# In the drain of a routed MoE pipeline, the down products of the last unit but one are put in front of the gate/up products of the last unit

## What is computed

```
xn = layernorm(x)
s  = RWKV attention(xn): three time-mixed projections, a scan over time, output product with Wo
# MoE with 16 experts, top 4, hidden size 256:
probs = softmax(xn @ w_router.T); top_w, top_e = top_k(probs, 4); top_w /= sum|top_w|
for e in range(16):
    h = silu(xn @ w_gate[e]) * (xn @ w_up[e])
    ffn += coeff_e * (h @ w_down[e])          # coeff_e = 0 where e isn't chosen
out = x + s * silu(ffn)
```

## Time and profile before

| | value |
|---|---|
| median of 3 runs | 324.53 us |
| the profiled execution | 324.29 us, span 322.5 us |
| PE busy | 287.6 us (89%) |
| DVE busy | 251.2 us (78%) |
| ACT busy | 146.0 us (45%) |
| POOL busy | 203.7 us (63%) |
| chain that ended last | PE 60%, DVE 16%, DMA 12% |

### The profile page before, as it was taken

How to read it: one execution, slowest core, us unless ns; L and a number is a source line. 1 busy time by engine, 2 the same in 40 slices (tenths; PEclk the granted TensorE clock), 3 DMA queues, 4 the chain that set the end, 5 groups by cost and what they waited for, 6 DMA issues and landing times.

```text
span 322.5 us, 4601 instructions
## 1 busy us (share of the span) xinstructions
PE 287.6 (89%) x1298; PEld 212.3 (66%) x1299; DVE 251.2 (78%) x523; ACT 146.0 (45%) x219; POOL 203.7 (63%) x201
## 2 busy tenths in 40 slices
PE   0698969979889999999999999999999999969960
PEld 0443424434335665888888888888888888848850
DVE  2889799986986888689299896898869961439993
ACT  1791726423267752841935536465273232312140
POOL 3600089993773767778778787787777776242281
PEclk9999979999999999999999999999999999988995
DMA  7896000016377676459655454655556578899798
GB/s 230 285 374 287 0 1 1 0 34 244 99 236 273 226 272 218 146 212 291 217 199 170 149 213 148 227 160 192 171 168 207 155 221 301 265 337 303 223 230 163
DMA packets 30379, 63.28 MB, mean 196 GB/s; under 512 B 4332, under 2 KB 20205, under 8 KB 30192
## 3 DMA queue, kind: packets, MB, share of 16 engines
q10 hardware_dynamic: 7568, 23.88, 21.2%
q0 software_dynamic: 8544, 19.41, 21.2%
q1 hardware_dynamic: 14240, 19.66, 18.1%
HBM read 50.35 MB, written 15.20 MB: 203 GB/s over the span
## 4 chain that ended last, share of the span: by engine, by line
PE 60%; DVE 16%; DMA 12%; issue 4%; ACT 3%; POOL 3%; ACTq 1%; SPq 0%; DVEq 0%; POOLq 0%
PE ps L589 52%; DMA rows<-wgu_in 5%; PE ps L696 4%; DVE arena L848 3%; DVE ohB L1007 2%; DMA y_rows<-arena,dst_idx 2%; PE ps L599 2%; DVE ohA L1002 2%; DMA wrou<-wrouT_in 1%; DMA rows<-y_rows 1%; DVE arena L1136 1%; DMA y_rows<-arena,late 1%; POOL arena L393 1%; POOL y_rows L400 1%; DVE arena L1103 1%
## 5 line engine op out<-in xcount | busy, mean ns | idle before, releaser
L589 PE MATMUL ps<-arena,rows 128*128 128x256 f32 x448 | 102.8, 384 | 3.1 <-DMA rows<-wgu_in 3.1
L393 POOL DMA_INDIRECT arena<-xn_rows,tok_idx x72 | 79.6, 1106 | 26.2 <-issue 21.6
L589 PEld LDWEIGHTS ps<-arena,rows 128*128 128x128 f32 x448 | 84.1, 193 | 13.9 <-issue 3.5
L400 POOL DMA_INDIRECT y_rows<-arena,dst_idx x60 | 65.2, 1086 | 26.2 <-issue 16.5
L589 PE MATMUL ps<-wdn,arena 128*128 x288 | 67.8, 380 | 0.4 <-DVE arena L1036 0.4
L589 PEld LDWEIGHTS ps<-wdn,arena 128*128 128x128 f32 x288 | 54.2, 191 | 7.7 <-issue 0.8
L589 PE MATMUL ps<-arena 128*128 128x512 f32 x96 | 47.1, 624 | 3.1 <-DVE arena L848 3.1
L549 ACT COPY arena<-ps 128x512 f32<-128x512 f32 x34 | 19.9, 586 | 63.9 <-PE ps L589 55.0
L375 POOL TENSOR_SCALAR ohB<-late 128x128 f16<-128x128 f32 x20 | 31.4, 1581 | 26.3 <-DVE late L924 26.3
L1036 DVE TENSOR_TENSOR arena<-arena,ps 128x512 f32<-128x512 f32 x28 | 19.1, 683 | 33.5 <-PE ps L589 15.3
L539 ACT ACTIVATE arena<-ps 128x512 f32<-128x512 f32 x36 | 21.5, 598 | 35.0 <-PE ps L589 34.9
(11 more groups left out here) (185 smaller groups left out, 370.9 us busy)
## 6 DMA issues: line engine op xcount, KB each, us to landing
rows<-wgu_in ACTq DMA_DIRECT2D x44, 512.0 KB, 3.9
rows<-y_rows SPq DMA_DIRECT2D x6, 768.0 KB, 7.2
wdn<-wd_in SPq DMA_DIRECT2D x1, 4096.0 KB, 14.9
rT<-x_in SPq DMA_DIRECT2D x4, 512.0 KB, 6.4
xn_rows<-rT SPq DMA_DIRECT2D x4, 512.0 KB, 3.3
rows<-y_rows SPq DMA_DIRECT2D x8, 256.0 KB, 4.9
out<-x_in SPq DMA_DIRECT2D x1, 1536.0 KB, 9.5
rows<-y_rows SPq DMA_DIRECT2D x3, 512.0 KB, 5.7
```

Of the source, the lines that this page charges most:

```text
L393: pool.indirect_dma_start(out=xg[i % XG][:, j, :], out_offset=None, in_=xn_rows, in_offset=bass.IndirectOffsetOnAxis(ap=tok_idx[:, 2 * i + ...
L400: pool.indirect_dma_start(out=y_rows, in_=ysb[:, par, j, :], in_offset=None, out_offset=bass.IndirectOffsetOnAxis(ap=idx[:, n + j:n + j + ...
L589: ins = nc.tensor.matmul(dst, lhsT(c), rhs(c), start=(c == 0), stop=(c == C - 1))
```

## The change

Three engines get another order in the drain. No instruction is added or dropped.

```
 ScalarE
-            silu(low + LAG - 1, (FIRST - 1) % 2)
             for n, (par, column) in enumerate(((FIRST % 2, 5), ((FIRST - 1) % 2, 5))):
+                if n == 1:
+                    silu(low + LAG - 1, par)
 TensorE
             optional(pe, blocks, step)
+            first = pe.value_load(used[0:1, 2:3], ...)
+            down_last(0, low + LAG - 2, FIRST % 2, expert_of(first + 2 * (LAG - 2)))
             loads = pe.value_load(used[0:1, 4:5], ...)
             gate_up(low + LAG - 1, (FIRST - 1) % 2, 2 + (FIRST - 1) % 2, loads)
-            first = pe.value_load(used[0:1, 2:3], ...)
-            down_last(0, low + LAG - 2, FIRST % 2, expert_of(first + 2 * (LAG - 2)))
             down_last(1, low + LAG - 1, (FIRST - 1) % 2, expert_of(first + 2 * (LAG - 1)))
 VectorE
-            for k in range(PARTS):
+            for k in range(2):
                 dve.wait_ge(y_first_in[k], 16)
                 summed(0, part[k])
             hidden(low + LAG - 2, FIRST % 2)
+            dve.wait_ge(y_first_in[2], 16)
+            summed(0, part[2])
```

More of the change, by code:

```diff
@@ L781, in _ @@
             optional(pe, blocks, step)
+            first = pe.value_load(used[0:1, 2:3], min_val=2 * (FIRST - LAG), max_val=2 * (NP - LAG))
+            down_last(0, low + LAG - 2, FIRST % 2, expert_of(first + 2 * (LAG - 2)))
             loads = pe.value_load(used[0:1, 4:5], min_val=16 * (NEED // 2 - 1), max_val=16 * (NP // 2 - 1))
             gate_up(low + LAG - 1, (FIRST - 1) % 2, 2 + (FIRST - 1) % 2, loads)
-            first = pe.value_load(used[0:1, 2:3], min_val=2 * (FIRST - LAG), max_val=2 * (NP - LAG))
-            down_last(0, low + LAG - 2, FIRST % 2, expert_of(first + 2 * (LAG - 2)))
             down_last(1, low + LAG - 1, (FIRST - 1) % 2, expert_of(first + 2 * (LAG - 1)))
```

## The result

The changed kernel takes 328.36 us (median of 20 runs, 325.0 to 333.63); beside it, the kernel before took 325.26 us (20 runs, 323.38 to 329.36). The ratio is 1.006, with a 95% interval of 1.0034 to 1.0087: slower by about 2.0 us (0.006 times 325.26). The ratio is the figure to go by: it compares only the runs within 1.5% of each kernel's fastest, while the medians of all runs are 3.1 us apart. Forecast were +2.4 us and a slower kernel at 0.77. Laid on the 324.53 us that the forecast started from, the ratio gives 326.5 us (325.6 to 327.4), in the forecast's own range of 326.3 to 327.8; rival C, 325.4 to 326.3, isn't excluded by the interval.

What follows compares the result with a forecast made beforehand. DVE was taken to set the end, with PE held by a far branch: 2.65 us later on PE less a 0.26 us wait gives +2.4, 324.29 to 326.7, so 326.9 us at the median; own range 326.3 to 327.8, 8-in-10 range 324.4 to 328.0.

Steps and rivals of the forecast that it cites:

- rival C: PE's clock isn't halved, or only up to 292.0: slower by less, +0.85 to +1.8, 325.4 to 326.3 us; chance 0.14.
- What bounds: DVE sets the end from 290.02 us; its only holes to 317.27 are 0.28 and 0.26 us.
- The branch: PE's third branch at L266 takes 6133 ns for a code fetch, ends at 288.1 again and holds whatever follows.
- The first down product: On PE, register loads and address arithmetic take 1.8 us behind the branch; first down matmul at 290.0 us.
- 24 matmuls and the clock: PE work before the product of n-1: 5.19 us at full clock plus 1.55 for half clock, 2.65 us later.
- The end: On DVE, the product of n-1 waits 2.65 us longer, a later 0.26 us wait goes: 2.4 us.
- A, the gap is used: PE's branch returns at once, or its wait was the weights': both DVE holes go, -0.54, 324.0 us; chance 0.08.
- B, even: PE's fetch usually takes a microsecond or so less, branch ending by 287.2 at full clock: 324.5 us; chance 0.13.
- E: Half clock outlasts 5 us, or DVE meets the late scatters of n-1: over 327.8 us; chance 0.04.
- What was said of DMA and ACT: Scatters moved forward (256 KB, 0.7 us of transfer) and ACT's silu of n-1 behind two copies cost nothing.

Runs made afterwards that it cites:

- all loads ahead: Changed kernel with TensorE's four drain register loads made ahead of the conditional blocks: 326.29 us, ratio 1.0012 to the kernel before.
- changed, both: Changed kernel with PE's register loads ahead of the conditional blocks and slot 1's third part ahead of the product of n-1 on DVE: 326.09 us, ratio 0.9988.
- before, loads ahead: Kernel before, with TensorE's drain register loads made ahead of the conditional blocks: 328.05 us, ratio 0.9999.
- matched pair: First profile of the kernel before and second of the unchanged changed kernel (one run, 327.21 us), with branches of 6.13 and 6.25 us.
- DVE's order alone: Kernel before with the changed order on DVE only, TensorE and ScalarE in the old order: 327.34 us, ratio 1.0027.
- the kernel with the near drain: Changed kernel with TensorE's program holding only the two conditional pairs that run, so no far branch: 323.77 us, ratio 0.9941.
- the old order with the near drain: Kernel before with TensorE's program holding only the two conditional pairs that run: 325.24 us, ratio 0.9973.
- PE's and ACT's order alone: Changed kernel with VectorE put back in the order before, TensorE and ScalarE in the changed order: 328.29 us, ratio 1.0078.

## Why the prediction was right

*What bounds.* Confirmed: DVE has no hole behind the product of n-1 and sets the end; the chain now says so by itself. But the 0.28 us ahead of that product, from which the forecast read that DVE's own order nearly held it, was a matter of that one profile: in the three others with PE's old order and the long branch PE held it, for 1.68, 2.73 and 4.31 us.

*The branch.* Confirmed, and it is the heart of it: it was 4.6 and 6.3 us in the changed kernel, nothing could start before it ended, and without it the order costs nothing that the runs show. The fetch that the forecast names is in the traces, as a packet of q8 in the branch. The forecast took its length for fixed; it is between 3.9 and 7.2 us in the ten profiles that have the one long jump. The sum doesn't hang on the length, as long as the weights have landed by its end; the time of a run does, which is why single profiles mislead.

*The first down product.* 1.8 us behind the branch were taken from the sequence in the earlier trace rows; 1.76, 2.08, 1.83 and 1.79 were found. By the earlier trace rows, the load group in front was priced at 0.9 us more than before; 0.7 to 1.1 was found. With all loads ahead about half a per cent of the time came back, 1.6 us, which fits the 1.4 to 1.7 us that they take in the timelines.

*24 matmuls and the clock.* 5.19 us at full clock: from the first down product to the product of n-1 it was 5.63 us in the profiles with a full clock, of which 0.39 was taken for the last step to DVE. With the clock halved, 7.21 us, 1.6 more (taken: 1.55). The reason given for the halving, that PE's pause is longer, isn't borne out as a rule: "changed, both" kept the full clock over a pause of 3.63 us and the first profile of the changed kernel over one of 2.36 us, while "before, loads ahead" was halved after one of 1.96 us. Where the clock was halved it cost 1.5 to 1.8 us with the old order and 1.6 to 2.8 us with the new one, so for the most part it cancels in the difference, as it does in the forecast (1.50 against 1.55 us). Whether it is halved equally often in both isn't known: four of four profiles had it with the old order and the long branch, and four of seven with the new order and a branch ahead of the drain's matmuls.

*The end.* +2.65 on PE less 0.26 for the wait that goes: 2.4. The matched pair gives 3.05 on PE's side (+16.86 less +13.81) and 2.7 at DVE's end; the ratio gives about 2.0. A reason for the smaller ratio that fits, but isn't shown: with the old order DVE later waits for slot loads, 0.26 us in the first profile, 0.88 in the second and 1.00 in "DVE's order alone" (none in "before, loads ahead"), and such waits take up a part of PE's delay. In the changed kernel's two profiles there are none. That the middle of the forecast is so near the ratio is in part luck: it stands on the waits of one profile.

*The rivals.* A, the gap is used, is what the kernel with the near drain shows: 0.6% faster than before, of which the old order with the near drain has 0.3%; what the order adds to it isn't settled. B, even, and C asked for a shorter branch and a full clock. Both came together in two profiles, the changed kernel's first one and "PE's and ACT's order alone", and there DVE ends sooner than in before (+35.81 and +35.18); over all runs the loss remained. E's long half clock came in one profile of a variant; its late scatters didn't.

*What was said of DMA and ACT* held: the scatters forward cost nothing that could be seen, and ACT's silu of n-1 wasn't late (in the near drain neither, where the product of n-1 waits for DVE's own work).

## What to carry to other kernels

An idle engine whose wait the chain puts down to a transfer may be held by its own sequencer as well: look for branches, register loads and packets of the instruction queue in that gap before you move work into it, for they show up in no busy share. Work moved in front of a late step only uses a gap if the engine can issue in it; behind a stall it is simply more work ahead of whoever waits. And lay two traces over each other from a common step near the change, not from zero, and take more than one profile where single stalls vary by 3 us.

## What the runs showed of the hardware

- A far taken branch on PE took 3.9 to 7.2 us, short taken ones 213 to 362 ns, one that falls through 65 to 89 ns. It started 4 us ahead of the end of PE's queued matmuls (282.0 against 286.0) and was still 2.1 us late.
- Each long branch has a 16 KB packet of an instruction queue 2.35 to 2.5 us ahead of its end (2.9 us in one profile); the rest of its length, 1.55 to 4.3 us, is the time up to that packet. A pause of 4.37 us without any branch, four matmuls behind a far branch, has such a packet 2.3 us ahead of its end.
- Jumps over some 129 instructions were long every second time, 5.7 and 5.9 us.
- On DVE, ACT and POOL the same construct cost 34 to 67 ns. Why it is short there, no run shows.
- A register load on PE took 300 to 420 ns, and a chain of two with its arithmetic 1.4 to 1.7 us behind a branch.
- In the drain, PE's granted clock was halved after pauses of 1.96 to 4.33 us in seven profiles and after one of 10.42 us in an eighth, and stayed full over pauses of 1.74, 2.36 and 3.63 us in three others.
